# Conditional adapter and layer norm: down products two tiles ahead, own columns and banks for the last pieces

## The chip, the cores and the metric

The kernel runs on one core of one Trainium2 chip. The metric is the device time of one execution, in microseconds (us). The median of three runs of the kernel before is 776.12 us (774.63 to 779.03).

## What is computed

The program is a chain of four conditioned layers over x of 64 batches by 64 tokens by 256 channels. Layers 0 and 1 (a quantised gated MLP; attention and a SwiGLU MLP) are untouched by the change. The change is in the last stage, which computes layers 2 and 3:

```
dWd = ((h_lang @ Wdd.T + bdd) * 0.1).reshape(B, 128, 256)
dWu = ((h_lang @ Wdu.T + bdu) * 0.1).reshape(B, 256, 128)
down = relu(einsum('bld,bnd->bln', x, Wd + dWd) + bd)
x = x + einsum('bln,bdn->bld', down, Wu + dWu) + bu
out = (x - mean) * rsqrt(var + 1e-5) * weight + bias
out = (out + tanh(cond @ lin_w.T + lin_b)[:, None, :]) * weight + bias
```

Each batch has adapter weights of its own. An earlier stage makes them (64 batches of 256 KB) and stores them to HBM as `adapter_w`; the last stage loads them back.

## The kernel before, in words

x stands in SBUF transposed, as [128 channels, 2 halves, 4096 tokens]. The last stage (`adapter_and_norm`) goes through it in nine pieces: pieces 0 to 6 are tiles of 512 tokens (8 batches), pieces 7 and 8 are the two halves of tile 7, of 256 tokens each. I write down(t), up(t) and so on for the step of piece t. The steps of a piece are:

- **down(t)**, TensorE (PE), L1751: x times the down weights, 64-column matmuls per batch, into bank 4. It waits for `slot_loaded` of its tile (all of the tile's weight loads) and for relu(t-1), since there is one bank.
- **relu(t)**, ScalarE (ACT), L1717: bank 4 into the SBUF buffer `inner` (a half of mlp_in). It waits for down(t) and up(t-1).
- **up(t)**, PE, L1774: `inner` times the up weights, into banks 7 and 0. Then the additions to x, VectorE (DVE), L1832, two per piece.
- **halves' sum(t)**, GpSimd (POOL), L1810: the two halves of x added into `x_sum`; **mean(t)**, PE, L1762 in `add_partitions`: a matmul with ones, into bank 1; **centre(t)**, DVE, L1860, two per piece, into one of three buffers (silu, g, centred).
- **squares(t)**, ACT, L1728, two per piece; their sum into `sq_sum`, POOL, L1805; **var(t)**, PE, L1762, into bank 2; **Ln and Exp(t)**, ACT, L1735 and L1737.
- **norm(t)**, DVE, L1843, two per piece; **shift(t)**, POOL, L1796, two per piece; **store(t)**, issued by SP, L1710, one per half.

For the last piece, both sums and one shift are on DVE (L1838, L1852, L1796). `sums`, the mean bank and the variance bank are single, so sums of piece 8 wait for the matmuls of piece 7.

The order on each engine is written out by hand: `pipeline` calls a body once per step s, in which piece s-1 does its up product, s its down product, s-2 its variance and s-3 its output. On PE a step is: up(s-1), down(s), var(s-2), mean(s-1).

SP's loop orders its queue. Weights of tiles 0 to 4 are loaded ahead of the stage (L1649). Tiles 5, 6 and 7 are loaded in four quarters each (L1642, 512 KB each), two quarters per step s = 1 to 6, into memory of weights that are done with by then. The first quarter of step s waits for s down products, the second for s up products, and from s = 3 on the stores of piece s-3 stand behind them. So the quarters of step 6 (the second half of tile 7) stand behind the two stores of piece 2. PE waits for 64 counts of `slot_loaded[7]`, that is for all four quarters, at down(7) and at down(8).

`ending["first_down"]` puts down(0) ahead of the last chunk of the MLP before it, whose result is read by DVE at L1554 from banks 5 and 6, and added to x at L1565 (`last_residual`).

Of the kernel before, what the change touches and what calls it, by code (L numbers as in the profile page):

```python
# [14 lines left out]
FP32 = mybir.dt.float32  # L15
# [717 lines left out]
def layers(nc, io, core, bank, keep, early, adapter_w, base_w, slot_loaded, out):  # L733
# [18 lines left out]
    with ExitStack() as c:  # L752
# [53 lines left out]
        ending = adapter_and_norm(nc, core, bank, sb, sem, S, (silu, g, spare), ya, adapter_w, slots, slot_loaded, out)  # L806
# [846 lines left out]
def adapter_and_norm(nc, core, bank, sb, sem, swiglu, xc, sq, adapter_w, slots, slot_loaded, out):  # L1653
# [9 lines left out]
    inner, log_var = core["mlp_in"][:, 0], core["mlp_in"][:, 1]  # L1663
# [4 lines left out]
             "norm_done out_done last_out stored prep").split()  # L1668
    S = {n: sem("d_" + n) for n in names}
    down_ps, up_ps, mean_ps, var_ps, rstd_ps = bank[4], (bank[7], bank[0]), bank[1], bank[2], (bank[3], bank[5])  # L1670
# [23 lines left out]
    def sync_program(sp):  # L1694
        for s in range(1, N + 3):
            if s <= 2 * (TILES - 5):
                tile, part = 5 + (s - 1) // 2, (s - 1) % 2
                sp.wait_ge(S["down_ready"], s)
                load_weight_rows(sp, adapter_w, slots, slot_loaded, tile, 2 * part)
                sp.wait_ge(S["up_ready"], s)  # L1700
                load_weight_rows(sp, adapter_w, slots, slot_loaded, tile, 2 * part + 1)
            if s >= 3:
                t = s - 3
                _, at, w = PIECES[t]
                for m in range(DH):
# [7 lines left out]
    def relu(act, t):  # L1713
        w = width(t)
        act.wait_ge(S["down_ready"], t + 1)
        wait(act, S["up_ready"], t)
        nc.scalar.activation(inner[:, 0:w], down_ps[:, 0:w], ACT.Relu, bias=vecs[:, V_BD:V_BD + 1]).then_inc(S["inner_done"], 1)  # L1717

    def scalar_program(act):
        nc.scalar.preload_act_table_set("natural_log_exp_and_others")  # L1720

        def body(s):
            if s.live(2):
                t, w = s.at(2), width(s.at(2))
                wait(act, S["sq_sum_done"], t)
                for m in range(DH):
                    act.wait_ge(S["xc_done"], DH * t + m + 1)
                    nc.scalar.activation(sq[:, m, 0:w], xc[t % 3][:, m, 0:w], ACT.Square).then_inc(S["sq_done"], 1)  # L1728
            if s.live(0) and not s.first():
                relu(act, s.at(0))  # L1730
            if s.live(2):
                t, k, w = s.at(2), s.at(2) % 2, width(s.at(2))
                act.wait_ge(S["var_ready"], t + 1)
                wait(act, S["norm_done"], DH * (t - 1))
                nc.scalar.activation(log_var[:, 0:w], var_ps[:, 0:w], ACT.Ln, scale=1.0 / D, bias=wscale[:, 2:3]).then_inc(S["ln_done"], 1)  # L1735
                act.wait_ge(S["ln_done"], t + 1)
                nc.scalar.activation(rstd_ps[k][:, 0:w], log_var[:, 0:w], ACT.Exp, scale=-0.5).then_inc(S["rstd_done"], 1)  # L1737
        act.wait_ge(swiglu["h_ready"], TILES)
        relu(act, 0)
        act.wait_ge(swiglu["ya_done"], DH * TILES)  # L1740
        act.wait_ge(S["prep"], 6)
        pipeline(act, N, 3, N, body)

    def down(pe, t):
        pe.wait_ge(slot_loaded[PIECES[t][0]], 32 if PIECES[t][0] < 5 else 64)
        pe.wait_ge(swiglu["x_done"], PIECES[t][0] + 1)
        wait(pe, S["inner_done"], t)
        for b, at in batches(t):
            for d in range(DH):
                for col in range(2):  # L1750
                    last = nc.tensor.matmul(down_ps[64 * col:64 * col + 64, at:at + L], weight(t, b, 0, d, col),  # L1751
# [13 lines left out]
    def tensor_program(pe):  # L1765
        def body(s):
            if s.live(1):
                t = s.at(1)
                pe.wait_ge(S["inner_done"], t + 1)
                wait(pe, S["x_done"], DH * t)  # L1770
                for m in range(DH):
                    for b, at in batches(t):
                        for col in range(2):
                            last = nc.tensor.matmul(up_ps[m][64 * col:64 * col + 64, at:at + L], weight(t, b, 1, m, col),  # L1774
                                                    inner[:, at:at + L], start=True, stop=True)
                last.then_inc(S["up_ready"], 1)
            if s.live(0):
                down(pe, s.at(0))
            if s.live(2):
                t, w = s.at(2), width(s.at(2))  # L1780
                pe.wait_ge(S["sq_sum_done"], t + 1)
                wait(pe, S["ln_done"], t)
                add_partitions(var_ps, sq_sum, w).then_inc(S["var_ready"], 1)
            if s.live(1):
                t, w = s.at(1), width(s.at(1))
                pe.wait_ge(S["x_sum_done"], t + 1)
                wait(pe, S["xc_done"], DH * t)
                add_partitions(mean_ps, x_sum, w).then_inc(S["mean_ready"], 1)
        pe.wait_ge(swiglu["g_done"], TILES * FC)
        pipeline(pe, N, 2, N, body, start=1)  # L1790
# [8 lines left out]
    def gpsimd_program(pool):  # L1799
        def body(s):  # L1800
            if s.live(2) and not s.last(2):
                t, w = s.at(2), width(s.at(2))
                pool.wait_ge(S["sq_done"], DH * (t + 1))
                wait(pool, S["var_ready"], t)
                nc.gpsimd.tensor_tensor(sq_sum[:, 0:w], sq[:, 0, 0:w], sq[:, 1, 0:w], ALU.add).then_inc(S["sq_sum_done"], 1)  # L1805
            if s.live(1) and not s.last(1):
                t, w = s.at(1), width(s.at(1))
                pool.wait_ge(S["x_done"], DH * (t + 1))
                wait(pool, S["mean_ready"], t)
                nc.gpsimd.tensor_tensor(x_sum[:, 0:w], piece(t, 0), piece(t, 1), ALU.add).then_inc(S["x_sum_done"], 1)  # L1810
            if s.live(3):
                t = s.at(3)
                for m in range(1 if s.last(3) else DH):
                    pool.wait_ge(S["norm_done"], DH * t + m + 1)
                    shifted(nc.gpsimd, t, m).then_inc(S["out_done"], 1)
# [111 lines left out]
```

## Time and profile before

| | before |
|---|---|
| median of three runs | 776.12 us |
| lowest, highest | 774.63, 779.03 us |
| the profiled execution | 775.45 us |
| its span, first to last instruction | 773.7 us |
| outside the span | 1.75 us |
| PE busy | 748.5 us (97% of the span) |
| DVE, POOL, ACT busy | 522.4, 426.8, 357.5 us |

Times in a trace are counted from the first instruction of the span. A timeline row says start, length, engine, line, operation, output and input, how many, and in brackets how long its engine was idle before it and what ended that. Lengths of merged rows run from the first start to the last end. Matmuls overlap in the pipeline, so a matmul's length is more than its share of a row of them. "PEclk" is the granted TensorE clock as a share of 2.4 GHz.

### The profile page before, as it was taken

How to read it: one execution, taken by the hardware profiler on the slowest of the kernel's cores; microseconds unless marked ns; L12 is line 12 of the kernel's file. 1: busy time of each engine (PE TensorE's matmuls, PEld its weight loads, DVE VectorE, ACT ScalarE, POOL GpSimd, SP SyncE). 2: the span in 40 equal slices, each digit the busy share in tenths (PEclk: the TensorE clock that was granted, in tenths of full speed). 3: DMA queues.
4: the chain of work that ended last, by engine and by line, in shares of the span. 5: the costliest groups of instructions: out<-in, count | busy, mean ns of one | idle time of the engine just before them, and what ended most of it. 6: DMA issues, size and time to landing. Idle time of an engine off the chain costs nothing.

```text
span 773.7 us, 18782 instructions
## 1 busy us (share of the span) xinstructions
PE 748.5 (97%) x6756; PEld 604.9 (78%) x6756; DVE 522.4 (68%) x768; ACT 357.5 (46%) x693; POOL 426.8 (55%) x418
## 2 busy tenths in 40 slices
PE   8999999999998999999989999999999999999894
PEld 7788888888887989999978676767676777688783
DVE  4877777777888988889864664646564646443465
ACT  4344444444457688888754333323232323222453
POOL 4655656564777899999976524232423232000476
PEclk9999999999999999999999999999999999999998
DMA  8945444444432100000004558677686767497473
GB/s 242 279 104 103 97 119 103 104 104 117 104 76 51 45 3 3 2 0 0 3 16 109 172 169 229 193 215 207 180 239 191 224 189 220 128 321 278 156 255 109
DMA packets 80810, 105.57 MB, mean 136 GB/s; under 512 B 39760, under 2 KB 53296, under 8 KB 80624
## 3 DMA queue, kind: packets, MB, share of 16 engines
q1 hardware_dynamic: 79600, 103.19, 46.8%
q10 hardware_dynamic: 1152, 1.59, 0.7%
q8 instruction: 40, 0.66, 0.3%
q14 instruction: 18, 0.15, 0.1%
HBM read 75.09 MB, written 21.26 MB: 125 GB/s over the span
## 4 chain that ended last, share of the span: by engine, by line
PE 88%; POOL 4%; DVE 3%; issue 2%; DMA 2%; SPq 1%; ACT 1%; POOLq 0%; ACTq 0%; DVEq 0%
PE banks L1177 23%; PE banks L434 21%; PE banks L1191 12%; PE banks L1028 4%; PE banks L1211 4%; PE banks L451 4%; PE banks L1105 3%; PE banks L1063 3%; PE banks L1146 3%; PE banks L1087 2%; PE banks L1762 2%; PE banks L1774 2%; PE banks L1121 2%; DMA early<-in_cond_w 2%; PE banks L1751 1%
## 5 line engine op out<-in xcount | busy, mean ns | idle before, releaser
L1541 DVE TENSOR_TENSOR g<-banks,silu 128x512 f32<-128x512 f32 x64 | 44.2, 690 | 90.1 <-PE banks L1177 45.4
L1375 ACT ACTIVATE silu<-banks 128x512 f32<-128x512 f32 x64 | 38.2, 597 | 105.4 <-PE banks L1177 105.4
L1545 DVE TENSOR_TENSOR g_lo<-g,g_hi 128x512 fp32r<-128x512 f32 x64 | 54.7, 855 | 45.9 <-ACT g_hi L1381 45.9
L1381 ACT ACTIVATE g_hi<-g 128x512 fp32r<-128x512 f32 x64 | 40.5, 632 | 95.9 <-DVE g L1541 94.9
L434 PE MATMUL banks<-up_hi,xs_hi 128*128 128x512 f32 x256 | 82.1, 402 | 2.6 <-POOL xs_lo L363 1.6
L1177 PE MATMUL banks<-mlp_in_hi,w_hi 128*128 128x512 f32 x256 | 81.0, 398 | 3.1 <-POOL mlp_in_lo L723 3.1
L1177 PE MATMUL banks<-mlp_in_lo,w_hi 128*128 128x512 f32 x256 | 80.3, 395 | 0.0
L1177 PE MATMUL banks<-mlp_in_hi,w_lo 128*128 128x512 f32 x256 | 80.2, 395 | 0.0
L434 PE MATMUL banks<-up_lo,xs_hi 128*128 128x512 f32 x256 | 79.4, 391 | 0.1
L434 PE MATMUL banks<-up_hi,xs_lo 128*128 128x512 f32 x256 | 79.2, 391 | 0.0
L658 DVE SCALAR_TENSOR_TENSOR h<-banks,rstd,gelu 128x512 f32<-128x512 f32 x64 | 47.9, 748 | 36.8 <-ACT gelu L554 36.5
L723 POOL TENSOR_TENSOR mlp_in_lo<-mlp_in,mlp_in_hi 128x1024 fp32r<-128x1024 f32 x8 | 19.7, 2468 | 81.9 <-ACT mlp_in_hi L730 81.9
L925 POOL TENSOR_TENSOR p_sb<-p_sb,rec 128x1024 f32<-128x1024 f32 x32 | 60.7, 1906 | 6.7 <-DVE rec L1500 6.6
L554 ACT ACTIVATE gelu<-banks,rstd 128x512 f32<-128x512 f32 x64 | 43.9, 687 | 43.7 <-PE banks L434 39.1
L1177 PEld LDWEIGHTS banks<-mlp_in_hi,w_hi 128*128 128x128 f32 x256 | 48.3, 190 | 14.8 <-issue 3.3
L1177 PEld LDWEIGHTS banks<-mlp_in_lo,w_hi 128*128 128x128 f32 x256 | 48.3, 189 | 11.5
L1177 PEld LDWEIGHTS banks<-mlp_in_hi,w_lo 128*128 128x128 f32 x256 | 48.3, 189 | 11.2
L434 PEld LDWEIGHTS banks<-up_lo,xs_hi 128*128 128x128 f32 x256 | 47.9, 188 | 11.1 <-DVE up_lo L693 0.9
L434 PEld LDWEIGHTS banks<-up_hi,xs_lo 128*128 128x128 f32 x256 | 48.1, 188 | 10.3
L434 PEld LDWEIGHTS banks<-up_hi,xs_hi 128*128 128x128 f32 x256 | 45.5, 188 | 11.9 <-POOL xs_lo L363 1.8
L1191 PE MATMUL banks<-g_hi,w_hi 128*128 128x512 f32 x128 | 54.3, 424 | 0.0
L713 POOL TENSOR_TENSOR mlp_in<-x_sb,stat 128x1024 f32<-128x1024 f32 (+1 forms) x8 | 19.5, 2434 | 61.0 <-DMA stat<-rstd_row 61.0
(200 smaller groups left out, 1827.3 us busy)
## 6 DMA issues: line engine op xcount, KB each, us to landing
gen_hyper<-in_gen_t SPq DMA_DIRECT2D x32, 512.0 KB, 4.6
gen_made<-base_w SPq DMA_DIRECT2D x64, 256.0 KB, 4.0
adapter_w<-gen_made SPq DMA_DIRECT2D x64, 256.0 KB, 3.1
tokens<-in_x_tok SPq DMA_DIRECT2D x32, 128.0 KB, 2.4
w_stage<-in_w_t SPq DMA_DIRECT2D x32, 128.0 KB, 2.4
tokens_again<-in_x_tok SPq DMA_DIRECT2D x32, 128.0 KB, 2.3
weight_slot<-adapter_w SPq DMA_DIRECT2D x4, 1024.0 KB, 9.1
x_sb<-in_x_t SPq DMA_DIRECT2D x7, 512.0 KB, 7.1
```

What stands on the lines that cost most here:

```text
L434: last = nc.tensor.matmul(bank[2 * j + part][:, :], (xs_hi, xs_lo)[a][:, k, d, :], up[b][:, d, at:at + 512], start=n == d == 0, stop=n == ...
L451: last = nc.tensor.matmul(y_ps, qt[:, s.slot(2, 2), f, :], downq[:, f, :], start=f == 0, stop=f == FC - 1)
L554: nc.scalar.activation(gelu[:, j, :], bank[2 * j + 1][:, :], ACT.Gelu, scale=rstd0[:, bass.ds(s.at(0), 1)]).then_inc(Z["gelu_done"], 1)
L658: nc.vector.scalar_tensor_tensor(out=h[:, k, j * 512:(j + 1) * 512], in0=bank[2 * j][:, :], scalar=rstd0[:, bass.ds(t, 1)], in1=gelu[:, j, ...
L925: nc.gpsimd.tensor_tensor(pu, pu, rec[:, two, :].unsqueeze(2).to_broadcast([P, 16, L]), ALU.mult).then_inc(A["norm_done"], 1)
L1028: last = nc.tensor.matmul(ps[:, m * GTA:(m + 1) * GTA], w1[a][:, w + d * D + m * P:w + d * D + (m + 1) * P], ha[b][k][:, d, :], start=n == ...
L1177: last = nc.tensor.matmul(bank[2 * (f % 2) + i][:, :], w1[a][:, at:at + P], hs[b][k][:, d, :], start=n == d == 0, stop=n == 2 and d == DH - 1)
L1191: last = nc.tensor.matmul(bank[5 + m][:, :], w1[a][:, at:at + P], gs[b][:, f % 2, :], start=f == n == 0, stop=f == FC - 1 and n == 2)
L1375: nc.scalar.activation(silu[:, f % 2, :], bank[2 * (f % 2)][:, :], ACT.Silu).then_inc(S["silu_done"], 1)
L1381: nc.scalar.activation(gs[0][:, f % 2, :], g[:, f % 2, :], ACT.Copy).then_inc(S["g_hi_done"], 1)
L1541: nc.vector.tensor_tensor(g[:, f % 2, :], bank[2 * (f % 2) + 1][:, :], silu[:, f % 2, :], ALU.mult).then_inc(S["g_done"], 1)
L1545: nc.vector.tensor_tensor(gs[1][:, f % 2, :], g[:, f % 2, :], gs[0][:, f % 2, :].bitcast(FP32), ALU.subtract).then_inc(S["g_ready"], 1)
```

## The change

Down products run two pieces ahead. For this there is a second bank (bank 6 for odd pieces) and a second `inner` (`other_inner`, laid over memory that the MLP is done with). down(t) waits for relu(t-2), relu(t) for up(t-2). down(1) writes bank 6, so it also waits until the MLP's result has been read from it. The second quarter of SP's step s waits for s-1 up products instead of s. The last piece gets the second half of `x_sum`, `sq_sum`, `sq` and `log_var`, and banks of its own for up, mean and variance. The order at the end is written anew: up(7) and up(8) in a row, then var(6), mean(7), mean(8), var(7), var(8); the squares of pieces 7 and 8 in a row; both shifts of piece 8 and one of piece 6 on DVE, the square sum of piece 8 on POOL. Nothing else of the program moves. The diff, cut to what sets order and waits:

```diff
-    inner, log_var = core["mlp_in"][:, 0], core["mlp_in"][:, 1]
+    inner, log_var = (core["mlp_in"][:, 0], other_inner), core["mlp_in"][:, 1]
...
-    down_ps, up_ps, mean_ps, var_ps, rstd_ps = bank[4], (bank[7], bank[0]), bank[1], bank[2], (bank[3], bank[5])
+    def down_ps(t):
+        return bank[6 if t % 2 else 4]
+    def up_ps(t, m):
+        return bank[(6, 4)[m] if t == LAST else (7, 0)[m]]
+    def mean_ps(t):
+        return bank[7 if t == LAST else 1]
+    def var_ps(t):
+        return bank[1 if t == LAST else 2]
...
-                sp.wait_ge(S["up_ready"], s)
+                sp.wait_ge(S["up_ready"], max(1, s - 1))
...
     def relu(act, t):
-        wait(act, S["up_ready"], t)
+        wait(act, S["up_ready"], t - 1)
...
         relu(act, 0)
+        relu(act, 1)
+        relu(act, 2)
...
+        for t in range(LAST - 1):
+            squares(t)
+            if t + 3 < N:
+                relu(act, t + 3)
+            rstd(t)
+        squares(LAST - 1)
+        squares(LAST)
+        rstd(LAST - 1)
+        rstd(LAST)
     def down(pe, t):
-        wait(pe, S["inner_done"], t)
+        wait(pe, S["inner_done"], t - 1)
+        if t == 1:
+            pe.wait_ge(swiglu["ya_done"], DH * TILES)
...
-        pipeline(pe, N, 2, N, body, start=1)
+        up(0)
+        down(pe, 1)
+        down(pe, 2)
+        means(0)
+        for t in range(1, LAST - 1):
+            up(t)
+            if t + 2 < N:
+                down(pe, t + 2)
+            variances(t - 1)
+            means(t)
+        up(LAST - 1)
+        up(LAST)
+        variances(LAST - 2)
+        means(LAST - 1)
+        means(LAST)
+        variances(LAST - 1)
+        variances(LAST)
...
+        add_squares(LAST - 1)
+        add_squares(LAST)
+        shift_out(LAST - 2, 0)
+        for m in range(DH):
+            shift_out(LAST - 1, m)
...
+        add_up(LAST - 1)
+        add_up(LAST)
+        nc.vector.tensor_tensor(x_sum[:, columns(LAST)], piece(LAST, 0), piece(LAST, 1), ALU.add).then_inc(S["last_step"], 1)
+        normalised(LAST - 3)
+        centre(LAST - 1)
+        centre(LAST)
+        normalised(LAST - 2)
+        shift_out(LAST - 2, 1)
+        normalised(LAST - 1)
+        normalised(LAST)
+        for m in range(DH):
+            shift_out(LAST, m)
```

PE in the middle of the stage, before: var(4), mean(5), up(6), then down(7), which waits for `slot_loaded7`. In these rows banks0 holds banks 0 and 1, banks1 holds 2 and 3, banks2 holds 4 and 5, banks3 holds 6 and 7.

```order
L1762 MATMUL banks1<-sums,ones 128x256 [waits d_ln_done,d_sq_sum_done]
L1762 MATMUL banks1<-sums,ones 128x256
L1762 MATMUL banks0<-sums,ones 128x256 [waits d_xc_done,d_x_sum_done]
L1762 MATMUL banks0<-sums,ones 128x256
L1774 MATMUL banks3<-mlp_in,w1_hi 64x64 [waits d_x_done,d_inner_done]
L1774 MATMUL banks3<-mlp_in,w1_hi 64x64 x7
L1774 MATMUL banks3<-mlp_in,w1_lo 64x64 x8
L1774 MATMUL banks0<-mlp_in,w1_hi 64x64 x8
L1774 MATMUL banks0<-mlp_in,w1_lo 64x64 x8
L1751 MATMUL banks2<-x_sb,w1_hi 64x64 [waits d_inner_done,m_x_done,slot_loaded7]
L1751 MATMUL banks2<-x_sb,w1_hi 64x64 x15
```

PE at the same place now: up(5), down(7), and only behind it var(4) and mean(5).

```order
L1802 MATMUL banks3<-other_inner,w1_hi 64x64 [waits d_x_done,d_inner_done]
L1802 MATMUL banks3<-other_inner,w1_hi 64x64 x7
L1802 MATMUL banks3<-other_inner,w1_lo 64x64 x8
L1802 MATMUL banks0<-other_inner,w1_hi 64x64 x8
L1802 MATMUL banks0<-other_inner,w1_lo 64x64 x8
L1781 MATMUL banks3<-x_sb,w1_hi 64x64 [waits d_inner_done,m_x_done,slot_loaded7]
L1781 MATMUL banks3<-x_sb,w1_hi 64x64 x15
L1792 MATMUL banks1<-sums,ones 128x256 [waits d_ln_done,d_sq_sum_done]
L1792 MATMUL banks1<-sums,ones 128x256
L1792 MATMUL banks0<-sums,ones 128x256 [waits d_xc_done,d_x_sum_done]
L1792 MATMUL banks0<-sums,ones 128x256
```

down(7) stood behind up(6); it now stands behind up(5), one step earlier, and var(4), mean(5) and up(6) stand behind it.

SP's queue around the loads of tile 7, now: the two stores of piece 1, the two step-5 quarters (w1_hi), the two stores of piece 2, the two step-6 quarters (w1_lo), and then stores.

```order
L1730 DMA out<-x_sb 128x512 [waits d_out_done] x2
L1643 DMA w1_hi<-adapter_w 128x2x512 [waits d_down_ready]
L1643 DMA w1_hi<-adapter_w 128x2x512 [waits d_up_ready]
L1730 DMA out<-x_sb 128x512 [waits d_out_done] x2
L1643 DMA w1_lo<-adapter_w 128x2x512 [waits d_down_ready]
L1643 DMA w1_lo<-adapter_w 128x2x512 [waits d_up_ready]
L1730 DMA out<-x_sb 128x512 [waits d_out_done] x7
```

Apart from the wait counts and the last four stores this order is the one before: the step-6 quarters did not move against the stores of piece 2.

PE's last rows before: down(8), var(6), mean(7), up(8), var(7), mean(8), var(8).

```order
L1751 MATMUL banks2<-x_sb,w1_lo 64x64 [waits d_inner_done,m_x_done,slot_loaded7]
L1751 MATMUL banks2<-x_sb,w1_lo 64x64 x15
L1762 MATMUL banks1<-sums,ones 128x256 [waits d_ln_done,d_sq_sum_done]
L1762 MATMUL banks1<-sums,ones 128x256
L1762 MATMUL banks0<-sums,ones 128x256 [waits d_xc_done,d_x_sum_done]
L1774 MATMUL banks3<-mlp_in,w1_lo 64x64 [waits d_x_done,d_inner_done]
L1774 MATMUL banks3<-mlp_in,w1_lo 64x64 x7
L1774 MATMUL banks0<-mlp_in,w1_lo 64x64 x8
L1762 MATMUL banks1<-sums,ones 128x256 [waits d_ln_done,d_sq_sum_done]
L1762 MATMUL banks0<-sums,ones 128x256 [waits d_xc_done,d_x_sum_done]
L1762 MATMUL banks1<-sums,ones 128x256 [waits d_ln_done,d_sq_sum_done]
```

PE's last rows now: up(7), up(8), var(6), mean(7), mean(8), var(7), var(8).

```order
L1802 MATMUL banks3<-other_inner,w1_hi 64x64 [waits d_x_done,d_inner_done]
L1802 MATMUL banks3<-other_inner,w1_hi 64x64 x7
L1802 MATMUL banks0<-other_inner,w1_hi 64x64 x8
L1802 MATMUL banks3<-mlp_in,w1_lo 64x64 [waits d_inner_done]
L1802 MATMUL banks3<-mlp_in,w1_lo 64x64 x7
L1802 MATMUL banks2<-mlp_in,w1_lo 64x64 x8
L1792 MATMUL banks1<-sums,ones 128x256 [waits d_ln_done,d_sq_sum_done]
L1792 MATMUL banks1<-sums,ones 128x256
L1792 MATMUL banks0<-sums,ones 128x256 [waits d_xc_done,d_x_sum_done]
L1792 MATMUL banks3<-sums,ones 128x256 [waits d_x_done,d_last_step]
L1792 MATMUL banks1<-sums,ones 128x256 [waits d_ln_done,d_sq_sum_done]
L1792 MATMUL banks0<-sums,ones 128x256 [waits d_xc_done,d_sq_sum_done]
```

down(8) has left this stretch for a place one step earlier, up(8) no longer waits for the additions of piece 7, and both means stand ahead of var(7).

## Rows read from the trace of the kernel before

**Rows 1.** The page, busy time by engine.

```profile
PE 748.5 (97%) x6756; PEld 604.9 (78%) x6756; DVE 522.4 (68%) x768; ACT 357.5 (46%) x693; POOL 426.8 (55%) x418
```

**Rows 2.** Busy by stretch: PE, PEld, DVE, ACT, POOL; PEclk, DMA share, GB/s.

```profile
716.00:719.00 3.00, 0.98 (x12) 0.74 (x7) 1.05 (x1) 0.69 (x1) 2.17 (x1) 1.00 0.86 270
719.00:722.50 3.50, 3.50 (x60) 3.07 (x60) 1.29 (x2) 1.23 (x2) 0.93 (x1) 0.51 0.15 53
722.50:766.00 43.50, 39.43 (x838) 33.08 (x835) 28.55 (x46) 21.92 (x37) 29.82 (x28) 1.00 0.54 183
766.00:773.70 7.70, 1.22 (x2) 0.50 (x2) 3.06 (x8) 1.58 (x4) 3.29 (x5) 0.56 0.39 136
```

**Rows 3.** Timeline of PE, start of the stage.

```profile
714.17 2.04 PE L1751 MATMUL banks<-x_sb,weight_slot 128*64 128x64 f32 x64
718.23 1.28 PE L1762 MATMUL banks<-sums,ones 128*128 128x256 f32 x4 [2.02 <-POOL sums L1810]
719.43 3.46 PE L1774 MATMUL banks<-mlp_in,weight_slot 128*64 128x64 f32 x64
```

**Rows 4.** Timeline of DVE and POOL, start of the stage.

```profile
712.36 1.41 DVE L1554 SCALAR_TENSOR_TENSOR y_alpha<-banks,vecs,cond_vectors 128x512 f32<-128x512 f32 x2 [2.88 <-PE banks L1191]
...
716.00 2.17 POOL L1810 TENSOR_TENSOR sums<-x_sb 128x512 f32<-128x512 f32 x1 [1.53 <-DVE x_sb L1832]
```

**Rows 5.** Timeline of PE, one step from up(4), and down(7).

```profile
738.83 2.08 PE L1774 MATMUL banks<-mlp_in,stat 128*64 128x64 f32 x64
740.75 1.10 PE L1751 MATMUL banks<-x_sb,w_hi 128*64 128x64 f32 x32
741.68 1.10 PE L1751 MATMUL banks<-x_sb,w_lo 128*64 128x64 f32 x32
742.72 2.20 PE L1762 MATMUL banks<-sums,ones 128*128 128x256 f32 x8
744.84 0.69 PE L1774 MATMUL banks<-mlp_in,w_hi 128*64 128x64 f32 x16
...
752.77 1.10 PE L1751 MATMUL banks<-x_sb,w_hi 128*64 128x64 f32 x32
```

**Rows 6.** Timeline of SP and POOL: stores of piece 2, step-6 quarters, shift(2).

```profile
744.76 1.36 SPq L1710 DMA_DIRECT2D out<-x_sb  x2
...
746.97 0.39 SPq L1642 DMA_DIRECT2D w_lo<-adapter_w  x1
...
743.68 2.05 POOL L1796 TENSOR_TENSOR x_sb<-centred,shift 128x512 f32<-128x512 f32 x2
```

**Rows 7.** Landing: all twelve of L1642; then the quarters issued at 746.97 and 746.16.

```profile
DMA to landing us min/median/max: 3.6/4.1/6.0
...
w_lo<-adapter_w SPq DMA_DIRECT2D x1, 512.0 KB, 5.7
...
w_lo<-adapter_w SPq DMA_DIRECT2D x1, 512.0 KB, 4.2
```

**Rows 8.** Timeline of PE, end of the stage: var(6) and mean(7), var(7) and mean(8), var(8).

```profile
760.33 1.56 PE L1762 MATMUL banks<-sums,ones 128*128 128x256 f32 x6 [1.38 <-POOL sums L1805]
...
764.31 1.13 PE L1762 MATMUL banks<-sums,ones 128*128 128x256 f32 x4 [1.34 <-POOL sums L1805]
767.69 1.22 PE L1762 MATMUL banks<-sums,ones 128*128 128x256 f32 x2 [2.25 <-DVE sums L1852]
```

**Rows 9.** Timeline of POOL, ACT and DVE, end of the stage.

```profile
763.54 0.72 POOL L1805 TENSOR_TENSOR sums<-y_alpha 128x256 f32<-128x256 f32 x1 [0.58 <-ACT y_alpha L1728]
...
768.95 0.47 ACT L1735 ACTIVATE mlp_in<-banks,wscale 128x256 f32<-128x256 f32 x1 [1.95 <-PE banks L1762]
769.46 0.39 ACT L1737 ACTIVATE banks<-mlp_in 128x256 f32<-128x256 f32 x1
...
769.88 0.87 DVE L1843 SCALAR_TENSOR_TENSOR centred<-centred,gain,banks 128x256 f32<-128x256 f32 x2 [2.24 <-ACT banks L1737]
770.78 0.55 DVE L1796 TENSOR_TENSOR x_sb<-centred,shift 128x256 f32<-128x256 f32 x1
```

More of the change, by code:

```diff
@@ L776, in layers @@
             spare = sb("centred", [P, DH, GTS], FP32, cx)
+            other_inner = sb("other_inner", [P, GTS], FP32, cx)
         for part, name in enumerate(("mlp_in_hi1", "mlp_in_lo1")):
@@ L1715, in relu @@
         act.wait_ge(S["down_ready"], t + 1)
-        wait(act, S["up_ready"], t)
-        nc.scalar.activation(inner[:, 0:w], down_ps[:, 0:w], ACT.Relu, bias=vecs[:, V_BD:V_BD + 1]).then_inc(S["inner_done"], 1)
+        wait(act, S["up_ready"], t - 1)
+        nc.scalar.activation(inner[t % 2][:, 0:w], down_ps(t)[:, 0:w], ACT.Relu, bias=vecs[:, V_BD:V_BD + 1]).then_inc(S["inner_done"], 1)
     def scalar_program(act):
         nc.scalar.preload_act_table_set("natural_log_exp_and_others")
[L1722 to L1737, printed above, removed]
@@ L1765, in tensor_program, with up @@
     def tensor_program(pe):
[L1766 to L1781, printed above, removed]
-                wait(pe, S["ln_done"], t)
-                add_partitions(var_ps, sq_sum, w).then_inc(S["var_ready"], 1)
-            if s.live(1):
-                t, w = s.at(1), width(s.at(1))
+        def up(t):
+            pe.wait_ge(S["inner_done"], t + 1)
+            wait(pe, S["x_done"], 0 if t == LAST else DH * t)
+            for m in range(DH):
+                for b, at in batches(t):
+                    for col in range(2):
+                        last = nc.tensor.matmul(up_ps(t, m)[64 * col:64 * col + 64, at:at + L], weight(t, b, 1, m, col),
+                                                inner[t % 2][:, at:at + L], start=True, stop=True)
+            last.then_inc(S["up_ready"], 1)
@@ L1786, in body, with variances, means @@
+        def variances(t):
+            pe.wait_ge(S["sq_sum_done"], t + 1)
+            if t == LAST:
+                pe.wait_ge(S["xc_done"], DH * LAST)
+            else:
+                wait(pe, S["ln_done"], t)
+            add_partitions(var_ps(t), sq_sum[:, columns(t)], width(t)).then_inc(S["var_ready"], 1)
+        def means(t):
+            if t == LAST:
+                pe.wait_ge(S["last_step"], 1)
+                pe.wait_ge(S["x_done"], DH * LAST)
+            else:
                 pe.wait_ge(S["x_sum_done"], t + 1)
@@ L1799, in gpsimd_program, with add_squares, add_halves, shift_out @@
     def gpsimd_program(pool):
[L1800 to L1815, printed above, removed]
+        def add_squares(t):
+            pool.wait_ge(S["sq_done"], DH * (t + 1))
+            wait(pool, S["var_ready"], LAST - 1 if t == LAST else t)
+            at = columns(t)
+            nc.gpsimd.tensor_tensor(sq_sum[:, at], sq[:, 0, at], sq[:, 1, at], ALU.add).then_inc(S["sq_sum_done"], 1)
+        def add_halves(t):
+            pool.wait_ge(S["x_done"], DH * (t + 1))
+            wait(pool, S["mean_ready"], t)
+            nc.gpsimd.tensor_tensor(x_sum[:, 0:width(t)], piece(t, 0), piece(t, 1), ALU.add).then_inc(S["x_sum_done"], 1)
+        def shift_out(t, m):
+            pool.wait_ge(S["norm_done"], DH * t + m + 1)
+            shifted(nc.gpsimd, t, m).then_inc(S["out_done"], 1)
         pool.wait_ge(swiglu["g_used"], TILES * FC)
```

109 lines of the change are left out of this document (63 added, 46 removed).

## The prediction

> **What bounds the kernel now.** I read the page first, then the busy time by stretch, then the timelines of PE, SP and POOL in the last 62 us, because the change touches nothing before 712 us. PE is busy 97% of the span [rows 1], and in the last stage too it sets the pace. One step there is up, down, var and mean: up(4) starts at 738.83 and up(5) at 744.84, so a step takes 6.01 us, and PE's rows join without a gap: 1.92 us for up, 1.97 for down, 2.12 for the eight matmuls of var and mean [rows 5]. In these steps an earlier down product can save nothing; PE has no idle time for it to fill. What there is to win lies at both ends of the stage.
>
> At the start PE stands idle 2.02 us, until POOL has summed piece 0 (POOL took 2.17 us) [rows 3, 4]. Behind this idle time the granted clock fell to 0.51, that is to 1.2 GHz, from about 719 to 722.5 us [rows 2], and up(1) took 3.46 us where up(4) took 2.08 [rows 3, 5]: 1.4 us more, and 1.5 with the slower end of mean(0) before it (1.20 us to the next start instead of 1.06). At the end PE waits 1.38, 1.34 and 2.25 us for sums of squares, and the last matmul runs at the lower clock, 1.22 us for two [rows 8]; the last stretch shows 0.56 [rows 2].
>
> **Start of the stage.** down(2) now stands behind down(1), from 716.1 to 718.1. POOL's sum ends at 718.17 [rows 4], so mean(0) starts at about 718.2 and the idle time is 0.1 us. With no idle time I expect no fall of the clock there. Gain: 2.02 - 0.1 + 1.5 = 3.4 us. The new wait of down(1), for the MLP's result to be read, costs nothing: DVE is done with it at 713.77 [rows 4], PE gets there at 714.17 [rows 3]. Its cover is 0.4 us. From here on PE has saved 3.4 us but has one more down product behind it (1.97), so up(5), which started at 744.84, starts at about 743.3, some 1.5 us earlier. The steps still take 6.01 us.
>
> **The load of tile 7.** This term decides. down(7) used to start at 752.77 [rows 5]. Its last quarter was issued at 746.97 and took 5.7 us to land [rows 6, 7], that is until about 752.65. The load was in time by 0.1 us. Now down(7) stands right behind up(5): PE wants it at 743.3 + 1.92 = 745.2 us. Are the quarters earlier too? SP issues them behind both stores of piece 2. These wait for shift(2) on POOL, which ended at 745.73 [rows 6] and which hangs on up(4) and var(2), which the change does not move against the step. It comes 1.5 us earlier with everything else, no more. So the second store goes out at 744.2, the first quarter at 744.6, and the second at 745.05; the relaxed count (5 up products, not 6) takes away only the 0.4 us between them. The nearest rows for the landing are 3.6 us as the least of twelve, 4.2 for a quarter with the same stores ahead of it, 5.7 for the one in question, 6.0 as the most [rows 7]. I take 5.0, between the last two by which it is nearest, since the two quarters now start together and share the queue: landed at 750.1, so PE waits 4.9 us at down(7) (3.4 to 6.0). var(4), mean(5) and up(6) stand behind it and wait as well; DVE, ACT and POOL run dry behind them.
>
> The Trainium skill, "DMA: Bandwidth & Descriptors", section "Anatomy of one DMA", gives a fit of about 2.0 us plus the bytes over 436 GB/s; for 512 KB that is an estimate of 3.2 us, below every landing in this trace. By it the wait would be 3.1 us and the total about 1.8 us lower than mine.
>
> Of the 4.9 us some 1.0 is not lost. Without the wait, var(4) and mean(5) would come too soon behind the shorter down(7) and would wait 0.55 and 0.4 us for POOL's sums; after a long wait these are there. Net 3.9 us.
>
> The other early loads hold: tile 5 is issued by 716.7 and needed at 733; tile 6's last quarter is issued at about 733.0 (the stores of piece 0 ahead of it) and lands by 738 to 738.7; down(6) wants it at 739.2. Cover 0.5 to 1.2 us.
>
> **The clock after that wait.** 2.02 us idle brought 3.4 us at 1.2 GHz and cost 1.5 us [rows 2, 3]. A wait of 4.9 us is more than twice as long, so I expect the same fall behind it, over down(7), var(4), mean(5) and perhaps up(6). From 0 (no fall) to 2.4 us (a stretch half as long again); I take 1.7. In the end piece PE again waits 1.5 and 1.9 us; before, 1.38 and 1.34 in a row did not bring the clock down, the time up to 766 shows 1.00 [rows 2, 8]. As the last matmuls ran at the lower clock before too, I add 0.4 (0 to 1.5).
>
> The Trainium skill, "TensorE: Matmul & The Clock Gate", section "What's actually happening", says the array runs at half rate once it has been idle and gets full rate back after sustained work; the trace agrees, with 0.51 behind the idle time at 716. It would make the wait at down(7) dearer, as taken here.
>
> **The end piece.** I laid out both orders step by step with the durations of the rows and the code's waits. The old order comes out at 773.85 for a span of 773.7, so the method holds. The new one without a wait at down(7) and at full clock: up(8) starts right behind up(7) at 756.3 and ends at 757.4; DVE has summed piece 8 at 759.0; var(6), mean(7), mean(8) run from 758.8 to 760.5; both centres are done at 762.2, the squares at 762.7; POOL adds two square sums of 0.72 us each [rows 9] until 763.5; var(8) ends at 764.1; two Ln and Exp pairs until 765.3, norm(8) until 766.2, two shifts of 0.55 until 767.2, and the store lands at 769.4. That is 4.5 us below 773.85: 3.4 of the start and 1.1 here. The gain here is small because var(8) still needs the whole chain of centre, squares and sum (the last wait was 2.25 us), and DVE now has the second shift of piece 8 (0.55) and one of 512 columns for piece 6, which no row of DVE shows; between 0.55 and 1.1 us, I took 0.85.
>
> **The sum**, against the profiled execution of 775.45 us (span 773.7 and 1.75 around it): -3.4 (start) - 1.1 (end piece) + 3.9 (wait for tile 7) + 1.7 + 0.4 (clock) = +1.5 us, 776.95 us. The median of the runs, 776.12, is 0.67 above that execution, so the forecast for a median is 776.12 + 1.5 = 777.6 us. About 0.5% (3.9 us) is what a measurement of this kernel can tell from no change; this is inside.
>
> **The rivals.**
> 1. *The wait comes, but cheap.* Quarters land in 3.6 us, the clock does not fall: +2.5 instead of +3.9 and nothing for the clock, so -2.0 us, 774.1. For it: the least landing. Against it: the two quarters behind two stores took 4.2 and 5.7. Still no change that can be told. Chance 0.12.
> 2. *No wait at down(7).* All of the 4.5 us is won, 771.6 us, faster. It needs the quarters within some 0.2 us of issue, or the stores of piece 2 far earlier than I work out, because shift(2) hangs on something else than I read. Against it: 0.1 us to spare before, one step less now. Chance 0.08.
> 3. *The clock does not come back.* The wait at down(7) drains the other engines, and PE waits 0.5, 0.4, 1.5 and 1.9 us in the 20 us behind it. If the clock stays at 1.2 GHz from 750 us to the end, every PE step doubles, and my layout ends at 783.1 where the old order ends at 773.85: +9.2, 785.3 us, slower. It decides from the point where the stretch at 0.5 is longer than some 8 us; before, it was 3.4 us. Chance 0.12.
> 4. *My forecast*, the wait of 4.4 to 5.7 us with one stretch at the low clock: 776.7 to 779.2. Chance 0.68.
>
> **How the numbers follow.** The likeliest case gives 777.6. The range takes in cases 4 and 1 with their bounds and about 1 us for the spread of runs (774.63 to 779.03): 773.0 to 781.0; case 2 and case 3 at full size stay out. Faster by over 0.5%: case 2, and a little of case 1, 0.09. Slower by over 0.5%: case 3 and the upper edge of 4, 0.14. Within 0.5%: 0.77.
>
> **What would show it.** The timeline of PE: no idle row at 716 to 718, up(1) in about 2.1 us, then a gap of 4 to 6 us ahead of down(7) (32 matmuls of 64 columns on w_hi), at about 745, with a DMA as the releaser. SP: the last w_lo quarter issued within 0.5 us of the one before, at about 745. The clock: 1.00 from 716 to about 748, then a stretch at 0.5. If there is no gap at 745, the reading of the stores as what holds the quarters is wrong; if the gap is there and the clock stays at 1.00, case 1 holds; if the time from down(7) to the end is over 28 us, case 3.

## The result, and the profile after

| | before | change |
|---|---|---|
| median | 776.38 us (17 runs) | 779.62 us (17 runs) |
| lowest, highest | 774.08, 779.65 us | 777.4, 786.53 us |
| ratio, 95% interval | | 1.0049 [1.003, 1.0068] |
| profiled execution, its span | 775.45, 773.7 us | 779.62, 777.7 us |
| up(0) to the end of the span | 61.41 us | 63.74 us |

The change is about 0.5% slower, and the interval lies wholly above 1. The last line of the table is the one that compares what the change touches: before, up(0), PE's row ahead of down(1), starts at 712.25; here it starts at 713.96. Of the 4.0 us between the two spans, 2.3 lie in the stage and 1.7 ahead of it.

Busy time, from the page, against [rows 1]. PE has 1.6 us more busy time for the same 6756 matmuls:

```profile
PE 750.1 (96%) x6756; PEld 606.0 (78%) x6756; DVE 526.8 (68%) x769; ACT 357.8 (46%) x693; POOL 426.9 (55%) x417
```

These 1.6 us all lie ahead of up(0), where PE was busy for 699.65 us before and is for 701.20 now. From up(0) to the end, before and then in the change, PE is busy for the same time at the same mean clock; the low clock has moved from the start of the stage to behind down(7), and the 2.3 us are idle time:

```profile
712.25:773.70 61.45, 48.88 (x1025) 41.13 (x1024) 36.85 (x60) 25.42 (x44) 38.11 (x39) 0.92 0.51 172
713.96:777.70 63.74, 48.86 (x1025) 41.28 (x1024) 38.13 (x61) 25.26 (x44) 37.17 (x38) 0.92 0.48 166
```

The stretches of the stage (PE, PEld, DVE, ACT, POOL busy, then PEclk, DMA share, GB/s), against [rows 2]. The fall of the clock has left 719 to 722.5, and a new one stands in 751 to 755, behind 6 us in which PE was busy for only 2.16:

```profile
719.00:722.50 3.50, 3.33 (x82) 2.81 (x78) 1.29 (x2) 1.26 (x3) 0.90 (x1) 1.00 0.88 270
...
745.00:751.00 6.00, 2.16 (x65) 1.95 (x64) 4.01 (x6) 1.60 (x3) 4.53 (x5) 0.90 0.79 260
751.00:755.00 4.00, 2.93 (x35) 2.64 (x36) 0.00 (x0) 0.47 (x1) 0.96 (x1) 0.50 0.39 147
755.00:766.00 11.00, 9.50 (x175) 7.71 (x173) 6.69 (x12) 5.39 (x9) 5.19 (x5) 0.92 0.13 49
```

PE's timeline of the stage: down(1), mean(0) and up(1), against [rows 3]; up(5), down(7), var(4) with mean(5), and up(6), against [rows 5]; the end, against [rows 8]. The idle time of 2.02 us at the start is now 0.17, and up(1) takes 2.09 us instead of 3.46.

```profile
715.88 2.04 PE L1781 MATMUL banks<-x_sb,weight_slot 128*64 128x64 f32 x64
...
719.95 1.13 PE L1792 MATMUL banks<-sums,ones 128*128 128x256 f32 x4 [0.17 <-POOL sums L1859]
721.01 2.09 PE L1802 MATMUL banks<-other_inner,weight_slot 128*64 128x64 f32 x64
...
745.07 0.69 PE L1802 MATMUL banks<-other_inner,w_hi 128*64 128x64 f32 x16
...
752.07 1.98 PE L1781 MATMUL banks<-x_sb,w_hi 128*64 128x64 f32 x32 [4.91 <-DMA w_lo<-adapter_w]
753.97 3.30 PE L1792 MATMUL banks<-sums,ones 128*128 128x256 f32 x8
757.21 0.69 PE L1802 MATMUL banks<-mlp_in,w_hi 128*64 128x64 f32 x16
...
760.67 1.13 PE L1792 MATMUL banks<-sums,ones 128*128 128x256 f32 x4 [0.45 <-POOL sums L1854]
762.15 1.13 PE L1792 MATMUL banks<-sums,ones 128*128 128x256 f32 x4 [0.35 <-POOL sums L1859]
...
766.68 2.00 PE L1792 MATMUL banks<-sums,ones 128*128 128x256 f32 x8 [1.38 <-POOL sums L1854]
770.67 1.48 PE L1792 MATMUL banks<-sums,ones 128*128 128x256 f32 x4 [1.99 <-POOL sums L1854]
```

up(5) starts at 745.07, which is 31.11 us behind up(0); before it was 32.59. So 1.48 us are won there. Then down(7) waits 4.91 us, and its releaser is a DMA of `w_lo`, the weights that down(7) does not even read. Behind it down(7) takes 1.98 us where [rows 5] had 1.10, and the eight matmuls of var(4) and mean(5) 3.30 instead of 2.20.

SP's queue at that place, against [rows 6]:

```profile
744.99 1.36 SPq L1730 DMA_DIRECT2D out<-x_sb  x2
746.39 1.96 SPq L1643 DMA_DIRECT2D w_lo<-adapter_w  x2
```

And the last quarter among the DMA issues (KB each, us from issue to landing), against [rows 7]:

```profile
w_lo<-adapter_w SPq DMA_DIRECT2D x1, 512.0 KB, 5.2
```

The quarters still start right behind the stores of piece 2, now in one go, and the last takes 5.2 us.

### The profile page after: what moved, and what is told of

It is laid out like the page before. It is cut to its first block, busy times and chain, and to the rows that moved or that the text cites. A ratio compares the mean times of both kernels' runs of the same rounds, so it can differ in the third digit from the quotient of the medians.

```text
span 777.7 us, 18780 instructions
## 1 busy us (share of the span) xinstructions
PE 750.1 (96%) x6756; PEld 606.0 (78%) x6756; DVE 526.8 (68%) x769; ACT 357.8 (46%) x693; POOL 426.9 (55%) x417
## 4 chain that ended last, share of the span: by engine, by line
PE 87%; POOL 4%; DVE 3%; DMA 2%; issue 2%; SPq 1%; ACT 1%; DVEq 0%; POOLq 0%; ACTq 0%
PE banks L1178 23%; PE banks L434 21%; PE banks L1192 12%; PE banks L1029 4%; PE banks L1212 4%; PE banks L451 3%; PE banks L1106 3%; PE banks L1064 3%; PE banks L1147 2%; PE banks L1088 2%; PE banks L1792 2%; PE banks L1122 2%; PE banks L1802 2%; DMA early<-in_cond_w 2%; PE banks L1781 1%
## 5 line engine op out<-in xcount | busy, mean ns | idle before, releaser
L1546 DVE TENSOR_TENSOR g_lo<-g,g_hi 128x512 fp32r<-128x512 f32 x64 | 57.6, 900 | 45.9 <-ACT g_hi L1382 45.9
```

The costliest lines, as they stand in the source:

```text
L1546: nc.vector.tensor_tensor(gs[1][:, f % 2, :], g[:, f % 2, :], gs[0][:, f % 2, :].bitcast(FP32), ALU.subtract).then_inc(S["g_ready"], 1)
```

## The experiments

Eight kernels. Each was run 12 times, in turns with the kernel before. All but one start from the changed kernel. Beside the ratio to the kernel before I give the time from up(0) to the end in the profiled execution, because the start of up(0) itself wandered between 710.85 and 716.10 us over the ten traces of this case.

| | median us | ratio, 95% | up(0) to end, us |
|---|---|---|---|
| before | 776.1 to 776.6 | 1 | 61.41 |
| change | 779.62 | 1.0049 [1.003, 1.0068] | 63.74 |
| 1 all loads early | 773.74 | 0.9964 [0.9944, 0.9985] | 58.64 |
| 2 before, loads early | 776.9 | 1.0008 [0.9988, 1.0028] | 61.95 |
| 3 down(7) waits for its half only | 772.86 | 0.9956 [0.9939, 0.9973] | 57.6 |
| 4 PE kept busy in the wait | 776.85 | 1.0014 [1.0, 1.0029] | 61.81 |
| 5 loads early, old end | 776.32 | 0.9997 [0.9975, 1.0019] | 62.02 |
| 6 loads early, shift on POOL | 774.4 | 0.9984 [0.9968, 0.9999] | 58.56 |
| 7 downs one ahead | 775.72 | 0.9985 [0.9964, 1.0005] | 59.09 |
| 8 quarters ahead of the stores | 777.83 | 1.001 [0.9991, 1.0029] | 62.29 |

### 1. All twelve quarters at the start of the stage

```diff
-            if s <= 2 * (TILES - 5):
-                tile, part = 5 + (s - 1) // 2, (s - 1) % 2
-                sp.wait_ge(S["down_ready"], s)
-                load_weight_rows(sp, adapter_w, slots, slot_loaded, tile, 2 * part)
-                sp.wait_ge(S["up_ready"], max(1, s - 1))
-                load_weight_rows(sp, adapter_w, slots, slot_loaded, tile, 2 * part + 1)
+            if s == 1:
+                for quarter in range(4 * (TILES - 5)):
+                    if quarter < 2:
+                        sp.wait_ge(S["down_ready"], quarter + 1)
+                    load_weight_rows(sp, adapter_w, slots, slot_loaded, 5 + quarter // 4, quarter % 4)
```

> The change, with all twelve quarters of tiles 5 to 7 issued in a row at the start of the stage, ahead of every store. My theory (the last quarters stand behind the stores of piece 2, and PE waits for them at down(7)): the gap of 4.9 us at down(7) and the stretch at 1.2 GHz behind it are gone; the time from up(0) to the end falls from 63.7 to about 57.5 us, and the kernel is 4 us (0.5%) under the kernel before, 772.4. Rival (the gap comes from the HBM or the queue being full, so earlier issue only moves the wait to another place): PE waits as long in all, and the time stays at 779 to 780.

Measured: 773.74 us, ratio 0.9964 [0.9944, 0.9985]. There is no gap at down(7) any more, and the clock stays up. PE's timeline, first beside the early loads, then down(7) and var(4):

```profile
732.86 0.51 PE L1801 MATMUL banks<-other_inner,gen_made 128*64 128x64 f32 x10
733.95 0.39 PE L1801 MATMUL banks<-other_inner,gen_made 128*64 128x64 f32 x6 [0.58 <-issue]
...
746.19 1.10 PE L1780 MATMUL banks<-x_sb,w_hi 128*64 128x64 f32 x32
747.75 1.13 PE L1791 MATMUL banks<-sums,ones 128*128 128x256 f32 x4 [0.45 <-POOL sums L1853]
```

The stretch from 745 us, with the clock at 1.00:

```profile
745.00:766.00 21.00, 15.18 (x268) 11.64 (x262) 16.52 (x29) 11.14 (x22) 15.90 (x16) 1.00 0.27 101
```

The load of tile 7 is what turned the change from a gain into a loss: taken away, the same order of work gains 0.36%. The moved loads have a price of their own: in 730 to 736 PE stands 0.58 us for "issue", at 727 another 0.20, and up(5) comes 32.1 us behind up(0) where it came at 31.11 in the change. Why PE stands there stays open.

### 2. The same loads in the kernel before

The edit is that of 1, in the kernel before.

> The kernel before, with the same early quarters. My theory: the load was in time by 0.1 us, PE never waited, so nothing changes: 1.000, within 0.2%. Rival (early loads are worth something by themselves, for instance less traffic beside the end): faster by 1 us or more. If moving 6 MB to the start delays the first steps, slower by 0.5 to 2 us.

Measured: 776.9 us, ratio 1.0008 [0.9988, 1.0028]. The early loads bring nothing by themselves, so the gain of 1 belongs to the new order. In this trace too they have a price: up(5) comes 33.1 us behind up(0), where it was 32.59 before. The stage starts as before, with PE's idle time ahead of mean(0) in its timeline:

```profile
716.81 1.22 PE L1761 MATMUL banks<-sums,ones 128*128 128x256 f32 x4 [2.01 <-POOL sums L1809]
```

And the clock falls as before; the stretch behind it:

```profile
717.80:721.00 3.20, 3.20 (x57) 3.04 (x58) 1.29 (x2) 1.23 (x2) 0.90 (x1) 0.50 1.06 407
```

### 3. down(7) waits for the half that it reads

down(7) and up(7) read `w_hi`, the step-5 quarters; `w_lo`, the step-6 quarters, is read by down(8) and up(8) alone. Here the second half is counted on a semaphore of its own (that of tile 0, long done), and only down(8) waits for it. No load moves.

```diff
-    ....then_inc(slot_loaded[t], 16)
+    ....then_inc(slot_loaded[0 if t == 7 and part else t], 16)
...
-        pe.wait_ge(slot_loaded[PIECES[t][0]], 32 if PIECES[t][0] < 5 else 64)
+        pe.wait_ge(slot_loaded[min(t, TILES - 1)], 32 if t < 5 or t >= TILES - 1 else 64)
+        if t == LAST:
+            pe.wait_ge(slot_loaded[0], 64)
```

> The change, with the second half of tile 7's weights counted on a semaphore of its own: down(7) waits for the two quarters it reads (step 5), down(8) for the other two. No load is moved. My theory: the step-5 quarters landed at 746.8 in the change's trace and PE wants them at 747.0, the step-6 ones at 752.0 and down(8) wants them about 753, so the gap is gone with the loads where they are: 772 to 774 us, like e1 or up to 1 us under it, since PE's waits on issue beside the twelve early loads (0.2 and 0.6 us) are not there. Rival (what e1 won came from moving the loads off the stores, not from PE's wait): stays near 779.

Measured: 772.86 us, ratio 0.9956 [0.9939, 0.9973], the fastest of all and faster than both kernels. PE's timeline from the end of up(5) on:

```profile
748.66 0.64 PE L1804 MATMUL banks<-other_inner,w_lo 128*64 128x64 f32 x16
749.13 1.10 PE L1783 MATMUL banks<-x_sb,w_hi 128*64 128x64 f32 x32
750.68 1.13 PE L1794 MATMUL banks<-sums,ones 128*128 128x256 f32 x4 [0.45 <-POOL sums L1856]
...
753.22 0.69 PE L1804 MATMUL banks<-mlp_in,w_hi 128*64 128x64 f32 x16
...
766.67 1.60 PE L1794 MATMUL banks<-sums,ones 128*128 128x256 f32 x4 [1.99 <-POOL sums L1856]
```

The stretch in which the change had its low clock:

```profile
751.00:755.00 4.00, 3.66 (x68) 2.84 (x68) 2.36 (x4) 2.18 (x4) 3.10 (x3) 1.00 0.78 255
```

The DMA issues: the quarter issued at 743.02 (for down(7)), then the one issued at 749.00 (for down(8)):

```profile
w_hi<-adapter_w SPq DMA_DIRECT2D x1, 512.0 KB, 5.8
...
w_lo<-adapter_w SPq DMA_DIRECT2D x1, 512.0 KB, 5.3
```

No wait at down(7). The quarter for it landed at 748.8, 0.3 us ahead of down(7)'s start; the one for down(8) at 754.3, 0.8 us ahead of its start at 755.13. The stage is 6.1 us shorter than in the change (57.6 against 63.74), and that is the price of the wait with all that hangs on it; the medians of the two kernels differ by 6.8 us. Against 1 it is 1.0 us shorter, which is what the early loads had cost.

### 4. PE kept busy while it waits

The wait stays, the clock is held: eighteen matmuls of the ones into the bank of down(7), ahead of its wait for the load.

```diff
+        wait(pe, S["inner_done"], t - 1)
+        if t == TILES - 1:
+            for i in range(18):
+                nc.tensor.matmul(down_ps(t)[:, 0:P], core["ones"][:], core["ones"][:], start=True, stop=True)
...
-        wait(pe, S["inner_done"], t - 1)
```

> The change, with 18 matmuls of ones with ones (128x128) into bank 6 ahead of down(7)'s wait for the load: some 4.8 us of work in place of the gap, nothing else moved. Their result is overwritten by down(7). My theory: the gap costs 4.9 us less the 1 us of slack, and the clock behind it 2.3 us more; the filler takes away only the 2.3: about 777.3, 1.001, with no stretch at 1.2 GHz between 745 and 766. Rival (the clock's part is not real or lies elsewhere): the same 779.6 as the change.

Measured: 776.85 us, ratio 1.0014 [1.0, 1.0029]. PE's timeline, with the added matmuls (the trace has two rows for each of them):

```profile
747.67 4.29 PE L1776 MATMUL banks<-ones 128*128 128x128 f32 x36
752.84 1.15 PE L1784 MATMUL banks<-x_sb,w_hi 128*64 128x64 f32 x32 [0.88 <-DMA w_lo<-adapter_w]
```

The stretches up to down(7) and behind its start:

```profile
745.00:753.70 8.70, 7.82 (x132) 7.20 (x132) 4.01 (x6) 2.15 (x4) 6.09 (x6) 1.00 0.78 273
753.70:770.00 16.30, 12.13 (x196) 9.42 (x192) 11.59 (x21) 8.52 (x16) 10.15 (x10) 1.00 0.21 76
```

down(7) still starts late, for the same load, but the clock shows 1.00 and down(7) takes 1.15 us instead of 1.98. The stage is 1.9 us shorter than in the change, and the median 2.8 us. So of what the wait cost, about a third was clock by the traces (1.9 of 6.1 us) and two fifths by the medians (2.8 of 6.8 us); the rest, 4.2 us in the traces, was the wait itself.

### 5. The old order at the end

With the loads of 1, so that no wait blurs the end: the last pieces' up, sums, squares and shifts in the order of before. Their own columns and banks stay.

```diff
-        up(LAST)
         variances(LAST - 2)
         means(LAST - 1)
-        means(LAST)
+        up(LAST)
         variances(LAST - 1)
+        means(LAST)
         variances(LAST)
```

(The same on SP, ACT, POOL and DVE, as in the kernel before.)

> As e1, but with the order of the end on every engine as before (banks and columns of the last piece stay its own). Measures the new end order. My theory: 3.4 us won at the start stay, the end gives back at most 1.1: 773 us, 0.9955. Rival (the new order at the end is what wins or what costs): over 1.5 us away from e1, to either side. In the trace of the change DVE's shift of 512 columns took 1.45 us where I had taken 0.85, so I hold it possible that e5 and e1 come out alike.

Measured: 776.32 us, ratio 0.9997 [0.9975, 1.0019], 2.6 us over 1, where my sum had 1.1. Here the clock fell within the end. PE's timeline at var(6) and mean(7):

```profile
760.38 2.93 PE L1789 MATMUL banks<-sums,ones 128*128 128x256 f32 x6 [2.31 <-POOL sums L1851]
```

The stretch over it:

```profile
760.30:763.50 3.20, 3.12 (x10) 2.11 (x12) 0.27 (x2) 0.97 (x2) 2.71 (x4) 0.50 0.20 75
```

The old order has a wait of 2.31 us ahead of var(6) and mean(7) where the kernel before had 1.38 [rows 8], because downs two ahead leave PE with less to do there; six matmuls then took 2.93 us instead of 1.56. So the new end is worth more under the new order than the 1.1 us that I counted from the old one. How much of the 2.6 us is order and how much clock is open. The stage of this one trace is 3.4 us over that of 1: the fall costs about 1.4 us of it (2.93 less 1.56), and 0.3 were lost before up(5), beside the early loads.

### 6. The second shift of piece 6 back on POOL

With the loads of 1. The suspect was DVE's shift of 512 columns, which the change adds.

```diff
-        shift_out(LAST - 2, 0)
+        for m in range(DH):
+            shift_out(LAST - 2, m)
...
-        shift_out(LAST - 2, 1)
```

(The first lines are POOL's, the last is DVE's.)

> e1, with the shift of piece 6's second half back on POOL. On DVE it took 1.45 us with POOL's shift beside it. My theory: norm(7) and norm(8) start 0.4 us earlier on DVE (they then wait for Exp instead), POOL ends 0.9 us later and its last stores become the end: within 0.5 us of e1, either side. Rival (this shift is what the end lost against my layout): 1 us or more under e1.

Measured: 774.4 us, ratio 0.9984 [0.9968, 0.9999]; 1 had 773.74, and the intervals overlap. No gain can be told. In the timeline of DVE and POOL in the change the shift takes 1.45 us, beside POOL's of 1.04 us, and the two shifts of 256 columns a little later, when POOL has nearly ended, take 0.78 us together:

```profile
771.36 1.04 POOL L1846 TENSOR_TENSOR x_sb<-silu,shift 128x512 f32<-128x512 f32 x1
771.50 1.45 DVE L1846 TENSOR_TENSOR x_sb<-silu,shift 128x512 f32<-128x512 f32 x1
...
774.44 0.78 DVE L1846 TENSOR_TENSOR x_sb<-centred,shift 128x256 f32<-128x256 f32 x2
```

I had taken 0.85. The 0.6 us more stand on the path that sets the end. The chain that ended last in 1 goes through the shift on DVE and from there into norm(7):

```profile
764.57 1.45 DVE x_sb L1845
766.02 0.78 DVE g L1896 x2
```

With the shift on POOL, here, the chain goes through the last matmuls and the Ln of piece 8 instead:

```profile
764.75 1.09 PE banks L1789 x2
765.87 0.48 ACT mlp_in L1749
```

The stages are nearly as long, 58.56 and 58.64 us, but the last four matmuls took 1.86 us here and 1.48 in 1, and they are now on the path. So the slower matmuls ate most of what the move had won in this trace. What the shift on DVE costs at equal matmul times is not shown.

### 7. Downs one ahead, all else as changed

```diff
-        down(pe, 2)
...
-            if t + 2 < N:
-                down(pe, t + 2)
+            down(pe, t + 1)
...
+        down(pe, LAST)
```

(ACT issues relu one piece ahead to match. The two banks and two `inner` stay.)

> The change with down products one piece ahead, as before, loads in the change's order, new order at the end kept. My theory: no wait at down(7), the idle time of 2.0 us and the slow clock at the start are back, so only the end is left: 0 to 1 us under before, 0.999 to 1.000. Rival (the loss of the change comes from the new end, not from the earlier down products): as slow as the change, 1.005.

Measured: 775.72 us, ratio 0.9985 [0.9964, 1.0005]; by the ratios that is 2.3 us over 3. PE's timeline at mean(0) and up(1):

```profile
720.79 1.13 PE L1790 MATMUL banks<-sums,ones 128*128 128x256 f32 x4 [2.01 <-POOL sums L1856]
721.86 2.09 PE L1800 MATMUL banks<-other_inner,weight_slot 128*64 128x64 f32 x64
```

The stretch behind it:

```profile
722.50:730.00 7.50, 7.50 (x194) 6.66 (x192) 3.46 (x7) 4.37 (x7) 2.55 (x2) 1.00 0.56 195
```

The idle time of 2.01 us is back, as it must be, but this time no fall of the clock came behind it. So the idle time does not bring the fall in every execution. This trace's stage, 59.09 us, is 1.5 over that of 3, and the runs say 2.3; with intervals of about 0.2% on either side these two can't be told apart, so how often the fall comes is not shown.

### 8. The step-6 quarters ahead of the stores of piece 2

```diff
-            if s <= 2 * (TILES - 5):
-                tile, part = 5 + (s - 1) // 2, (s - 1) % 2
+            for step in range(s, s + 1 if s < 5 else 7 if s == 5 else s):
+                tile, part = 5 + (step - 1) // 2, (step - 1) % 2
```

(In the loop's body `step` stands for `s`.)

> The change, with only one exchange in SP's queue: the two step-6 quarters go out right behind the step-5 ones, ahead of the stores of piece 2. My theory: they are issued at about 741 to 742 instead of 746.4 and 746.9 and share the queue with the step-5 quarters; 2 MB at some 300 GB/s from 741 are in at about 748, so the gap at down(7) shrinks from 4.9 to 1 to 2 us, and the time to 774 to 776. Rival (the queue is the limit, not the order): the gap stays over 3 us.

Measured: 777.83 us, ratio 1.001 [0.9991, 1.0029], and a gap of 4.12 us: my own expectation failed, the rival's held. SP's queue:

```profile
740.42 1.88 SPq L1643 DMA_DIRECT2D w_hi<-adapter_w  x2
742.35 0.98 SPq L1643 DMA_DIRECT2D w_lo<-adapter_w  x2
```

The last quarter among the DMA issues:

```profile
w_lo<-adapter_w SPq DMA_DIRECT2D x1, 512.0 KB, 8.4
```

PE's timeline at down(7):

```profile
751.33 1.98 PE L1781 MATMUL banks<-x_sb,w_hi 128*64 128x64 f32 x32 [4.12 <-DMA w_lo<-adapter_w]
```

The last quarter was issued some 4 us earlier, but with three other quarters ahead of it in the queue it took 8.4 us instead of 5.2. Only 0.8 us of the gap went. The stage is 1.5 us shorter than in the change, since var(4) and mean(5) behind down(7) took 2.65 us instead of 3.30. What took the gap away in these runs was to load far earlier (1) or not to wait for what is not read (3).

## Why the prediction was right

I forecast 777.6 us (773.0 to 781.0) and no difference that could be told as the likeliest. 779.62 us came out: in the range, 0.4 us above the 776.7 to 779.2 of the forecast's own case, and 3.2 us above the kernel before where I had 1.5. The mechanism is the one that I forecast, a wait at down(7) for the load and one stretch of low clock behind it. The 0.5% that I took as the least that a measurement can tell was too coarse: the interval reaches 0.2% to either side, and the slowdown is clear of it. Step by step:

- **Start of the stage.** Idle 0.1 us and a gain of 1.5 us by up(5): measured 0.17 and 1.48. The clock stayed at 1.00. That the fall behind the old idle time belongs to every execution was too much: it is in the traces of before and of experiment 2, and not in that of 7.
- **The load of tile 7.** "PE waits 4.9 us at down(7)": 4.91. The last quarter took 5.2 us (taken 5.0). That the order of the stores sets its issue was right, but 8 shows that the queue comes right behind: ahead of the stores it lands hardly earlier. The Trainium skill, "DMA: Bandwidth & Descriptors", section "Anatomy of one DMA", gives 2.0 us plus bytes over 436 GB/s, an estimate of 3.2 us for a quarter; it is a fit for GpSimd's path and for one transfer, and with others in flight the rows here show 5.2, 5.3, 5.8 and 8.4 us.
- **What is not lost of it.** I took 1.0 us; the two waits for POOL that experiment 3 has behind down(7) and the change has not are 0.45 and 0.34, together 0.8.
- **The clock after the wait.** I took 1.7 us. From down(7)'s start to up(6)'s the change needs 5.14 us and experiment 3 4.09, of which 0.79 is waiting: 5.14 - 3.30 = 1.84. Experiment 4 says the same in another way (1.9 in the trace, 2.8 in the medians). The Trainium skill, "TensorE: Matmul & The Clock Gate", section "What's actually happening", has the array at half rate once it has been idle; the row of 751 to 755 agrees with 0.50, and the idle time of 7, with 1.00 behind it, shows that an idle time need not bring it.
- **The end piece.** down(7) to the end without a wait was laid out as 24.2 us (745.2 to 769.4), and 0.4 added for the slower last matmuls; experiment 3 has 24.6. That the total fits so well is partly luck. Counted from down(7)'s start, the Exp of piece 8 ended after 20.1 us, just as laid out, although the last matmuls were slower (1.48 to 1.86 us for four in the traces with the new end and downs two ahead, 2.25 in 7, 1.13 at the full clock). The DVE shift was mis-sized, 1.45 us for 0.85, and it is on the path (experiment 6): norm(8) ended after 21.4 us where I had 21.0. The two last shifts took 0.78 us where I had 1.1, and the last store 2.5 where I had 2.2.
- **The sum.** -3.81 us for the new order without the wait (experiment 3: 57.6 against 61.41) and 6.14 for the wait make +2.33, where I had -4.1 and +5.6, +1.5. The 0.8 us between them are 0.2 of the waits for POOL, 0.15 of the clock, 0.15 of the longer wait (5.08 us from where down(7) would have started), and 0.25 of my layout of the old order ending at 773.85 for 773.7 and of rounding.
- **What the sum does not hold.** The medians differ by 3.2 us, the stage of the two traces by 2.3. The profiled pair differs by 1.7 us ahead of the stage as well, where the program is the same, and this arises at one place. PE comes out of a wait of 3.1 us for POOL at 395.26 us before and at 395.53 in the change, with the clock at 0.50 behind it in both. The next group of transposes (L1105, now L1106) starts at 403.43 and 405.14, and the 0.3 us between the traces have become 1.7. A stretch between the two, before:

```profile
398.50:401.50 3.00, 3.00 (x73) 2.31 (x73) 0.16 (x1) 0.79 (x2) 2.90 (x3) 1.00 0.02 5
```

The same stretch in the change:

```profile
398.50:401.50 3.00, 3.00 (x30) 1.96 (x33) 0.04 (x1) 0.00 (x0) 2.90 (x3) 0.50 0.00 0
```

From the end of that wait to that group the change takes 9.6 us, 4 and 7 take 9.5, the six others beside 2 take 8.2 to 8.4, and 2, where the clock stayed at 1.00 behind the same 3.1 us of waiting, takes 6.8. The program is the same there in all ten, so the difference comes and goes between executions, and no trace shows it to be an effect of the change. Over the runs the mean granted clock is 0.9882 for the change (17 runs) and 0.9900 for the kernel before (the 35 runs beside experiments 1, 2, 5 and 7). By my estimate this is up to 1.4 us (0.0018 of 777 us); where in the span it is lost, and whether it is more than chance, stays open.

The rivals: "no wait at down(7)" fell at once, and experiment 3 shows what it would have been worth (3.2 us in the medians). The cheap wait fell on both of its conditions: the landing took 5.2 us for 3.6, and the clock fell to 0.50. The clock did come back: 0.92 over 755 to 766, and down(7) to the end took 25.6 us, under the 28 that would have spoken for rival 3.

## What to carry to other kernels

When a product is moved a step ahead, look at its loads before its banks: its wait may ask for more than the product reads, and splitting that wait, with nothing moved, was worth 6.1 us in the trace where moving the transfer inside the same queue was worth 1.5 (experiment 8). A wait of some us on TensorE can be dearer than it is long: here 4.9 us cost 6.1, 1.8 of it as clock. Judge a term by a twin of the kernel without the wait, and by the stage rather than the span, where the span wanders by more than the term.

## What was not expected of the hardware

- The same idle time of 2.0 us at the same place lowered the clock in two traces (before, and experiment 2) and not in a third (experiment 7). A wait of 3.1 us at 395 us lowered it in nine traces and not in that of experiment 2.
- The same 512 KB took 3.6 to 6.0 us to land in the kernel before, where two quarters go out per step, and 8.4 with three others ahead in experiment 8.
- Six megabytes of loads in a row left PE standing for "issue" 0.20 and 0.58 us, and up(5) came 1.0 us later against up(0), with no wait of PE for a load in the profile.
- A DVE addition of 512 columns took 1.45 us beside POOL's, while two of 256 took 0.78 together. The Trainium skill, "GPSIMD Engine Reference", section "1. Specifications", says that GpSimd shares its SBUF interfaces with VectorE and that instructions of DVE with two SBUF inputs contend for them; the rows of experiment 6 agree: DVE's shift started 0.14 us behind POOL's and ended 0.55 us behind it.
